# Routed layers whose tails load the experts' rows of the first 512 tokens, normalise them and round the next stage's first weights, with no barriers between the six stages

## What is computed

```python
x = L0_attn_x                                     # (1, 2048, 256)
x = x + 0.5 * _L0_ffn_ref(_layernorm(x, axis=-1), ...)   # stage routed0
x = x + _L0_attn_ref(_layernorm(x, axis=-1), ...)        # stage attention0, one head
x = x + 0.5 * _L0_ffn_ref(_layernorm(x, axis=-1), ...)   # stage routed1
x = x + 0.5 * _L1_ffn_ref(_layernorm(x, axis=-1), ...)   # stage gated0
x = x + _L1_attn_ref(_layernorm(x, axis=-1), ...)        # stage attention1, 16 heads
x = x + 0.5 * _L1_ffn_ref(_layernorm(x, axis=-1), ...)   # stage gated1
```

```python
    eout = jnp.einsum('eci,eih->ech', mid, w_down) * wbuf[..., None]
    y = jnp.zeros((T + 1, h), x.dtype).at[buf.reshape(-1)].add(eout.reshape(-1, h))[:T]
    shared = jax.nn.silu(x @ sw_gate) * (x @ sw_up) @ sw_down
    return (y + shared).reshape(b, s, h)
```

## Time and profile before

| | us |
|---|---|
| median of 3 runs | 2043.96 (2040.21 to 2044.92) |
| the profiled execution: its time, its span | 2039.38, 2037.6 |
| PE, DVE, ACT, POOL busy | 1951.3, 1423.7, 1317.5, 947.1 |
| routed0, attention0, routed1, gated0 end near | 129, 260, 373, 493 |

### The profile page before, as it was taken

One profiled execution on the slowest core, in us unless ns is written; L12 is line 12 of the kernel. 1 busy time (PEld: TensorE's weight loads), 2 busy tenths in 40 slices (PEclk: granted clock), 3 DMA queues, 4 the chain that ended last, 5 costly groups with the idle time before them and its releaser, 6 DMA issues. The chain is left out here.

```text
span 2037.6 us, 40489 instructions
## 1 busy us (share of the span) xinstructions
PE 1951.3 (96%) x13831; PEld 1766.5 (87%) x13831; DVE 1423.7 (70%) x3588; ACT 1317.5 (65%) x3368; POOL 947.1 (46%) x974
## 2 busy tenths in 40 slices
PE   6988989898999999999999999999999999999899
PEld 4767867687899999999999999999999999998788
DVE  8348763545868777786877778787777878777653
ACT  4335633444778687777867777787777778777652
POOL 1642116534455536454553645545365454636242
PEclk9999999999999999999999999999999999999999
DMA  7752057700000000000000000000000000000010
GB/s 251 215 83 32 33 166 211 156 10 9 9 6 9 9 6 4 7 9 9 6 9 6 4 6 9 9 7 9 6 4 7 9 9 7 9 6 1 2 47 32
DMA packets 58602, 73.46 MB, mean 36 GB/s; under 512 B 9760, under 2 KB 45216, under 8 KB 58272
## 3 DMA queue, kind: packets, MB, share of 16 engines
q1 hardware_dynamic: 43808, 53.83, 8.2%
q0 software_dynamic: 14592, 17.04, 5.0%
HBM read 51.06 MB, written 19.80 MB: 35 GB/s over the span
## 5 line engine op out<-in xcount | busy, mean ns | idle before, releaser
L1184 ACT ACTIVATE phase_p<-phase_scores,phase_bias 128x512 f32<-128x512 f32 (+3 forms) x680 | 417.5, 628 | 117.0 <-DVE phase_bias L1172 116.3
L1230 DVE TENSOR_TENSOR phase_pt_lo<-phase_ring,phase_pt_hi 128x512 fp32r<-128x512 f32 (+3 forms) x680 | 390.3, 603 | 89.6 <-ACT phase_pt_hi L1225 85.8
L1225 ACT ACTIVATE phase_pt_hi<-phase_ring 128x512 fp32r<-128x512 f32 (+3 forms) x680 | 342.9, 536 | 106.2 <-PE phase_ring L1210 102.1
L1210 PE MATMUL phase_ring<-sb_ident,phase_p 128*128 128x128 f32 x2312 | 340.8, 274 | 10.8 <-ACT phase_p L1184 4.5
L160 PE MATMUL phase_y<-phase_pt_hi,phase_v_hi 128*128 128x256 f32 (+1 forms) x1152 | 341.5, 296 | 6.6 <-DVE phase_y_lo L2293 6.6
L161 PE MATMUL phase_y<-phase_pt_lo,phase_v_hi 128*128 128x256 f32 (+1 forms) x1152 | 321.5, 279 | 0.0
L162 PE MATMUL phase_y<-phase_pt_hi,phase_v_lo 128*128 128x256 f32 (+1 forms) x1152 | 321.4, 279 | 0.0
L1210 PEld LDWEIGHTS phase_ring<-sb_ident,phase_p 128*128 128x128 f32 x2312 | 272.2, 141 | 51.0 <-ACT phase_p L1184 14.0
L1165 DVE TENSOR_REDUCE phase_peaks<-phase_scores 128x1 f32<-128x512 f32 (+1 forms) x408 | 265.6, 665 | 46.3 <-PE phase_scores L1152 43.8
L2316 POOL TENSOR_TENSOR phase_straight<-phase_rot,late_rope 64x512 f32<-64x512 f32 x128 | 163.7, 1279 | 274.4 <-ACT phase_rot L2188 274.3
L2333 POOL TENSOR_TENSOR sb_x<-sb_x,phase_part 128x512 f32<-128x512 f32 x128 | 164.8, 1288 | 253.5 <-ACT phase_part L2223 247.1
(11 more groups left out here) (272 smaller groups left out, 4857.4 us busy)
## 6 DMA issues: line engine op xcount, KB each, us to landing
phase_e_up<-expert_up SPq DMA_DIRECT2D x32, 352.0 KB, 4.8
phase_e_dn<-expert_down SPq DMA_DIRECT2D x32, 256.0 KB, 5.4
y_rows<-phase_zero SPq DMA_DIRECT2D x16, 512.0 KB, 7.7
sb_x<-y_rows POOLq DMA_DIRECT2D x16, 512.0 KB, 6.6
xn_rows<-phase_ln_xn SPq DMA_DIRECT2D x8, 512.0 KB, 2.9
late_raw_qk<-qk SPq DMA_DIRECT2D x16, 256.0 KB, 2.6
sb_x<-x SPq DMA_DIRECT2D x4, 512.0 KB, 5.7
phase_raw_up<-up SPq DMA_DIRECT2D x8, 256.0 KB, 4.5
```

The lines of the kernel that those rows point to most:

```text
L1184: act.activation(self.p[:, at:at + width], self.scores[:, at:at + width], ACT.Exp, bias=self.bias[:, t % 2:t % 2 + 1], accum_out=self.sums ...
L1210: done = pe.transpose(bank[:, j * P:(j + 1) * P], self.p[:, (4 * place + j) * P:(4 * place + j + 1) * P], self.core.ident[:])
L1225: act.activation(hi, value, ACT.Copy).then_inc(*self.t_hi.one)
L1230: dve.tensor_tensor(lo, value, as_f32(hi), ALU.subtract).then_inc(*self.t_lo.one)
```

## The change

All six stages now go into one Block, so no barrier stands between them. In its place each engine of routed1, gated1 and attention1 waits for the last instructions of the stage before that matter (`follow`: TensorE for ScalarE and VectorE, and for GpSimd too in attention1; the other engines for all). Attention0 and gated0 wait for none of these as a whole.

Behind a routed stage's last expert SyncE loads the next stage's first weights, then rows 0 to 511 of both tables into SBUF rooms (two loads of 512 KB). VectorE adds them to chunk 0 (`grow` 0 and 1), in order before piece 10's and piece 11's `round`; it measures the chunk before piece 11's `round`, scales it behind half-sum (2,0), and TensorE turns it behind the last half-sum. ScalarE, VectorE and (for gated0) GpSimd round the next stage's first weights in the same tail (`ahead`). GpSimd's transfers of chunk 0 are gone, and the six others start with chunk 1. The matmuls without use at the first and third border are gone. In attention0 `values` 0 to 3 come earlier and chunk 1 is turned one tile earlier; in gated0 the side work comes one piece earlier.

```diff
+def follow(engine, prior, *ends):
+    for name in (ends or prior.ends) if prior else ():
+        engine.wait_ge(*prior.ends[name])
...
+        self.y_rooms = [self.e_up[:].rearrange("p s k w -> p (s k w)")[:, b * 4 * H:(b + 1) * 4 * H].rearrange("p (a h) -> p a h", a=4) for b in range(2)]
+        self.y_fetched, self.grown = [core.loads(f"y_fetched{b}") for b in range(2)], sig("grown")
...
+        self.first = ChunkNorm(core, sb, then, (0,), after=lambda c: self.grown[tag, 1], like=self.norm, quick=(0,))
+        self.first_banks = [banks[:, b, :] for b in (6, 7)]
...
-        fill(len(shared))
+        last = NCH * ISM - 1
+        among = {("up", last - 3): [("ahead", 0)], ("round", last - 3): [("ahead", 1)], ("up", last - 2): [("ahead", 2)],
+                 ("round", last - 2): [("ahead", 3)], ("gate", last): [("grow", 0)], ("up", last): [("grow", 1), ("measure",)],
+                 ("sums", NCH - 2, 0): [("scale",)], ("sums", NCH - 1, 1): [("flip", 0), ("flip", 1)]}
+        for steps in shared:
+            for step in steps:
+                order += [step, *among.get(step, ())]
         return order
...
+        self.follower.sp_ahead(sp)
+        sp.wait_ge(*self.e_downed[tag, NE - 1])
+        for b in range(2):
+            sp.wait_ge(*self.placed[b][tag, NE - 2 + b])
+            sp.dma_start(self.y_rooms[b], core.y_rows[b][0:CH, :].rearrange("(t p) h -> p t h", p=P)).then_inc(*self.y_fetched[b].one)
...
+            elif what == "ahead":
+                self.follower.act_ahead(act, *key)
+            elif what == "scale":
+                self.first.act_rows(act, 0)
+            elif what == "flip":
...
+            elif what == "ahead":
+                self.follower.dve_ahead(dve, *key)
+            elif what == "grow":
+                b, x = key[0], core.x[:, 0:4, :]
+                dve.wait_ge(*self.y_fetched[b][tag])
+                dve.wait_ge(*(self.grown[tag, 0] if b else self.added[tag, 0, 1]))
+                dve.tensor_tensor(x, x, self.y_rooms[b], ALU.add).then_inc(*self.grown.one)
+            elif what == "measure":
+                self.first.dve_stats(dve, 0)
+            elif what == "scale":
+                self.first.dve_rows(dve, 0)
+            elif what == "flip":
+                self.first.dve_rest(dve, 0, key[0], self.first_banks[key[0]])
+        self.step.totals[0] += self.steps
...
-        for half, c in GROWN[:3]:
-            if half == 0:
-                pool.wait_ge(*self.added[tag, c, 1])
-            pool.wait_ge(*self.placed[half][tag, NE - 2 + half])
-            pool_grow(core, pool, self.then, half, c)
-GROWN = ((0, 0), (0, 1), (1, 0), (1, 1), (0, 2), (1, 2), (0, 3), (1, 3))
+        self.follower.pool_ahead(pool)
+        pool.wait_ge(*self.y_fetched[0][tag])
+        self.pool_grow(pool, 0)
+        self.first.pool_inverse(pool, 0)
+        pool.wait_ge(*self.placed[1][tag, NE - 1])
+        self.pool_grow(pool, 1)
+    def pool_grow(self, pool, n):
+        half, c = GROWN[n]
+        pool.wait_ge(*self.added[self.tag, c, 1])
+        pool_grow(self.core, pool, self.then, half, c)
...
-    IDLE = {("flip", 0, 0): 22, ("state", 0): 6, ("score", 0, 0, 0): 9, ("score", 0, 1, 0): 5}
...
-        order = [("stats", 0), ("inverse", 0), ("grow", 3), ("grow", 4), ("rows", 0), *project(0)[:2], ("weights", "ws"),
-                 ("weights", "wa"), *project(0)[2:], ("stats", 1), ("weights", "wo0"), ("inverse", 1),
+        order = [("grow", 2), *project(0)[2:], ("values", 0), ("values", 1), ("stats", 1), ("inverse", 1), ("grow", 3), ("bias", 0),
                  ("score", 0, 0, 0), ("peak", 0, 0), ("exp", 0, 0)]
         for t in range(NT + 1):
             nc = t // 4 + 1
             if nc < NCH and t % 4 == 0:
-                order.append(("rows", nc))
-            order += {1: [("grow", 5)], 2: [("grow", 6)], 3: [("stats", 2), ("inverse", 2), ("grow", 7)], 6: [("stats", 3), ("inverse", 3)]}.get(t, [])
+                order += [("rows", nc), ("bias", nc)]
+            order += {1: [("grow", 4)], 2: [("grow", 5)], 3: [("stats", 2), ("inverse", 2)], 6: [("stats", 3), ("inverse", 3)]}.get(t, [])
...
-            if nc < NCH and t % 4 == 1:
+            if nc < NCH and t % 4 == (nc > 1):
                 order += project(nc)[:2]
-            if nc < NCH and t % 4 == 2:
+            if nc < NCH and t % 4 == 1 + (nc > 1):
                 order += project(nc)[2:]
-            if t < NT and t % 2 == 0:
+            if t in (2, 3):
+                order.append(("values", t))
+            if 8 <= t < NT and t % 2 == 0:
                 order.append(("values", t // 2))
...
+    def sp_ahead(self, sp):
         for name in self.names:
             sp.dma_start(self.raw[name], self.core.src[name]).then_inc(*self.weights_in[name].one)
...
+    def act_ahead(self, act, n):
+        if n < len(self.names):
+            name = self.names[n]
+            act.wait_ge(*self.weights_in[name][self.tag])
+            act.activation(self.w_hi[name][:], self.raw[name], ACT.Copy, scale=self.scale(name)).then_inc(*self.weight_hi.one)
...
+    def dve_ahead(self, dve, n):
+        if n < len(self.names):
+            name = self.names[n]
+            dve.wait_ge(*self.weight_hi[name])
+            dve.scalar_tensor_tensor(self.w_lo[name][:], self.raw[name], self.scale(name), as_f32(self.w_hi[name][:]),
+                                     ALU.mult, ALU.subtract).then_inc(*self.weight_lo.one)
...
-                pool_grow(self.core, pool, self.tag, *GROWN[step[1]])
-            elif step[0] == "rows":
+                self.prior.pool_grow(pool, step[1])
...
-            if step in self.IDLE:
-                core.keep_warm(pe, self.y[:], self.IDLE[step])
...
+        act.activation(self.spare[:], self.core.ident[0:1, 0:1], ACT.Exp)
...
-    GROW = {(0, 1): 5, (0, 2): 6, (0, 4): 7}
-    GROWN_NORM = {(0, 2): [("scale", 0, 1)], (0, 3): [("turn", 0, 1)], (1, 1): [("scale", 0, 2)], (1, 2): [("turn", 0, 2)],
-                  (1, 4): [("scale", 0, 3)], (1, 5): [("turn", 0, 3)]}
-    GROWN_LATE = {(0, 5): [("measure", 0, 2), ("invert", 0, 2)], (1, 2): [("measure", 0, 3), ("invert", 0, 3)]}
+    GROW = {(0, 0): 4, (0, 2): 5}
+    GROWN_NORM = {(0, 1): [("scale", 0, 1)], (0, 2): [("turn", 0, 1)], (1, 0): [("scale", 0, 2)], (1, 1): [("turn", 0, 2)],
+                  (1, 3): [("scale", 0, 3)], (1, 4): [("turn", 0, 3)]}
+    GROWN_LATE = {(0, 4): [("measure", 0, 2), ("invert", 0, 2)], (1, 1): [("measure", 0, 3), ("invert", 0, 3)]}
...
+    def sp_ahead(self, sp):
+        for m in range(I1M):
+            self.sp_up(sp, m)
+    def sp_up(self, sp, m):
+        sp.dma_start(self.raw_up[:, :, self.cols(m)], self.core.src["up1"][:, :, self.cols(m)]).then_inc(*self.up_in[m].one)
+    def sp_scales(self, sp):
...
     def sp(self, sp):
         core, src = self.core, self.core.src
-        for m in range(2 if self.ahead else 0, I1M):
-            sp.dma_start(self.raw_up[:, :, self.cols(m)], src["up1"][:, :, self.cols(m)]).then_inc(*self.up_in[m].one)
-            if m == 2:
...
         if self.add_y:
+            self.sp_scales(sp)
             sp.wait_ge(*self.norm.x_in[1][self.tag])
+            follow(sp, self.prior, "pe")
+        else:
+            follow(sp, self.prior)
+            for m in range(2, I1M):
+                self.sp_up(sp, m)
+                if m == 2:
+                    self.sp_scales(sp)
...
-        bank = self.down_ps[:, 0, :]
-        if 0 in self.ahead:
-            self.core.keep_warm(pe, bank, 6)
-        else:
-            self.core.keep_warm(pe, bank, 20)
-            self.pe_turn(pe, 0, 0)
-            self.core.keep_warm(pe, bank, 5)
+        if not self.add_y:
+            follow(pe, self.prior, "act", "dve")
+            self.core.keep_warm(pe, self.down_ps[:, 0, :], 6)
...
+    def act_ahead(self, act, m):
+        self.act_up_weights(act, m)
+    def dve_ahead(self, dve, m):
+        if m < 2:
+            self.dve_up_weights(dve, m)
+    def pool_ahead(self, pool):
+        for m in range(2, 4):
+            self.pool_up_weights(pool, m)
+    def pool_up_weights(self, pool, m):
+        pool.wait_ge(*self.up_w_hi[self.tag, m])
+        pool.tensor_tensor(self.up_lo[:, :, self.cols(m)], self.raw_up[:, :, self.cols(m)], as_f32(self.up_hi[:, :, self.cols(m)]),
+                           ALU.subtract).then_inc(*self.up_w_lo_p.one)
...
         if self.add_y:
-            pool_grow(self.core, pool, tag, *GROWN[3])
-        if not self.ahead:
-            self.norm.pool_inverse(pool, 0)
-            pool.wait_ge(*self.norm.powered[tag, 0])
-        if self.add_y:
-            pool_grow(self.core, pool, tag, *GROWN[4])
-        for m in range(2, I1M):
...
-            if m == 3 and not self.ahead:
-                self.norm.pool_inverse(pool, 1)
+            self.prior.pool_grow(pool, 2)
+            self.prior.pool_grow(pool, 3)
+            self.norm.pool_inverse(pool, 1)
+        else:
+            follow(pool, self.prior)
```

(17 more changed lines are left out.)

178 lines of the change are left out of this document (103 added, 75 removed).

## The result

The changed kernel takes **2045.32 us** (median of 12 runs) where the kernel before takes 2041.08 beside it (12 runs): the ratio is 1.002, 95% interval 1.0011 to 1.0028. So it is about 4 us **slower**; 11.5 us less was forecast, and the range ended at 2042. Its profiled execution took 2045.33 us, with a span of 2043.4, which is 5.8 more than before's 2037.6.

The account below looks back on a forecast made before the run. TensorE was taken as the bound, busy 1951.3 of 2037.6 us. Terms 0.75 + 4.5 + 5.1 + 1.4 + 1.7 - 1.7 = 11.75, forecast as 11.5 off the 2043.96 median, gave 2032.5 us; range 2026 to 2042.

Parts of the forecast that it names:

- Barriers: At the second, fourth and fifth border: a direct wait instead of a barrier saves 0.25 us each, 0.75 us.
- The first border's chain: From routed0's last scatters to attention0's first product: moved into the tail, product at 133.75 instead of 138.11, gain 4.4 us.
- rival 1: Both tails: the new loads take 6.6 us like the accumulating ones, giving 2040.4 us; chance 0.14.
- The stall at half-sum (3,0): In the tail: TensorE, queued behind VectorE's additions and measuring, waits a new 2.3 us.
- Rival 4: Both tails: late loads stop VectorE's ordered steps and TensorE behind; at 10.5 us a load, 2048.2 us; chance 0.07.
- The gain through attention0: Chunk 1's wait and chain end move up by about 4 to 5 us; 4.5 us taken for the first border.
- Rival 2: First border's gain is given back within attention0, chunk 2's rows still being added one after the other; 2037.0 us; chance 0.17.
- The rule on VectorE and GpSimd: Third tail: GpSimd's rounding could hold `grow` 0 by at most 1.1 us; nothing charged; as a rival 2033.6 us, chance 0.06.
- Lowered clock: In the two tails: idle time without the matmuls lowers the clock in one of them, minus 1.7 us (0 to 3.4).
- The third border: gated0's first product at 378.1 instead of 381.51, 3.4 us; with down weights issued earlier, gain 5.1 us there.
- chunk 3: In gated0: the 3.82 us wait before its turns falls to 2.4, gain 1.4 us, and 1.7 of lowered clock is spared.
- The four signs of being wrong: Loads over 5 us, stall at half-sum (3,0) over 4 us, half clock in more than one more stretch, attention0 no shorter.

Follow-up runs that it names:

- apart: Changed kernel with GpSimd's chunk 0 bias addition ahead of chunk 1's measuring, and its rounding behind routed1's last request for rows; 2047.25 us, ratio 1.0017.
- warm: Changed kernel with matmuls without use put back before half-sum (3,0) in two tails and in attention0; 2045.38 us, ratio 1.0012.
- after: The changed kernel itself, against the kernel before; 2045.32 us, ratio 1.002.
- late: Changed kernel with the next stage's weights requested only behind the last expert's down products; 2043.08 us, ratio 1.0002.
- chunk1: apart plus chunk 1 measured, inverted and scaled ahead of chunk 0's values in attention0; 2042.03 us, ratio 1.0010.
- cold6: best6 without the matmuls without use put back in the first three stages; 2037.94 us, ratio 0.9987.
- best6: best4 plus gated0's chunk 1 scaling one piece earlier and its down weights requested earlier; 2031.77 us, ratio 0.9962.
- best: Changed kernel with late, apart and chunk1 together and VectorE's additions placed where their rows land; 2041.17 us, ratio 0.9993.
- bestwarm: best plus some matmuls without use before each tail's first turns and in attention0; 2037.17 us, ratio 0.9980.
- third: Changed kernel with the first border and attention0 put back as before the change; 2041.32 us, ratio 1.0001.
- best4: best2 plus matmuls without use at routed1's opening, and GpSimd's rounding started once chunk 0's rows are scaled; 2034.58 us, ratio 0.9958.
- order: Changed kernel with VectorE's two additions, measuring and scaling moved behind half-sum (2,1)'s addition; 2053.68 us, ratio 1.0048.
- best2: bestwarm with GpSimd's rounding waiting until chunk 0's shift is written in the tail; 2033.69 us, ratio 0.9961.

## Why the prediction was wrong

In the profiles the forecast (11.75 us less before rounding) and the result (5.8 more) are 17.5 us apart. The difference has three large parts, beside small ones of either sign: 8.2 us up to attention0's first product, 3.3 more from there to chunk 1's state, and 6.2 behind gated0's first product, from which to attention1's 107.2 us would follow from the forecast and 113.4 were measured.

- **Barriers: right where it can be seen.** VectorE's last addition in attention0 ends at 267.49 + 0.48 = 267.97 and TensorE goes on at 268.12, 0.15 later (before 0.39). The fifth can't be told: attention1's first product to gated1's takes 1441.96 us instead of 1442.20, and 1441.2 to 1443.3 over the study.

```profile
267.49 0.48 DVE L1581 SCALAR_TENSOR_TENSOR sb_x<-phase_y,phase_inv,sb_x 128x256 f32<-128x256 f32 x1 [1.35 <-PE phase_y L172]
```
```profile
268.12 0.40 PE L170 MATMUL phase_banks<-sb_xt_hi,kept_w_hi 128*16 128x512 f32 x1 [0.67 <-DVE sb_x L1581]
```

- **The first border's chain: the step that cost most, wrong by 8.2 us** (141.97 instead of 133.75; 138.11 before). Its terms: expert 15's load was issued 2.1 us later, by chance as far as the profiles tell; the scatters came another 2.5 later, of which about 1.8 is the weights' request. The step that failed there counted the weights' roundings and put at nothing **SyncE's new loads, in a stretch where the transfer engines were already 89 to 98% busy** (98 to 104 us before the change). After the change the windows read (the last but one number is the DMA share; before, it was 0.04 from 104 to 106):

```profile
102.00:104.00 2.00, 1.86 (x9) 0.98 (x7) 0.48 (x1) 0.50 (x3) 0.67 (x2) 1.00 1.02 304
104.00:106.00 2.00, 1.64 (x9) 1.40 (x10) 0.34 (x1) 0.68 (x3) 1.08 (x1) 1.00 0.85 265
106.00:108.00 2.00, 2.00 (x14) 1.66 (x13) 0.00 (x0) 0.62 (x2) 0.00 (x0) 1.00 0.91 192
```

From the last scatter to the landing of the odd rows took 10.3 us instead of 8.0 (8.3 in apart and warm): 6.0 until the load could be issued, for which 4.4 was forecast, and 4.2 for the load. From there to the product took 13.6 instead of 12.3, above all since half-sums (3,0) and (3,1) ran mostly at half clock (6.6 us instead of 4.1). The loads themselves took 4.2 us, 0.7 over the estimate: rival 1 is out. The chain as such works, for with the clock at full it took 20.7 us from the last scatter (warm), 20.2 were forecast.
- **The stall at half-sum (3,0): mis-sized.** 6.03 us instead of 2.3. Its end hangs on the odd rows: (3,0) starts 4.4 us behind their landing in every run with this order (after, late, apart, chunk1; forecast: 4.6), since VectorE's addition of them and the measuring stand ahead of what TensorE needs. Rival 4 had that mechanism but priced only slow loads; the scatters ahead of them were late too.
- **The gain through attention0: wrong by another 3.3 us.** I expected chunk 1's wait and the end of its chain to move up by about the same 4 to 5 us. From first product to chunk 1's state took 19.1 instead of 15.8 us. That is GpSimd's bias addition, moved right behind chunk 1's power, holding a 128x4 step (shown by apart: 15.7). Without it the order still keeps 4 us: the values now stand ahead of the measuring of rows that had long landed (shown by chunk1: 11.6). Rival 2 had the gain given back in attention0, but by chunk 2's rows; from chunk 1's state to routed1's first product took only 1.2 us more than before.
- **The rule on VectorE and GpSimd: weighed, and priced at the wrong place.** The Trainium skill, SBUF — State Buffer, section Who interferes with whom, says that a VectorE instruction with two SBUF inputs and a GpSimd instruction that reads SBUF contend. The trace agrees, and shows the size: VectorE's step ends when GpSimd's instruction does (152.52 + 3.48 = 156.00, 153.11 + 2.86 = 155.97), so the short step pays for the long one. I took 1.1 us from a 256-wide subtraction and looked only at the third tail. There GpSimd's rounding ended before the rows landed, as I said, but it held a 128x512 subtraction of VectorE for 3.26 us (at 367.51; 0.66 elsewhere).
- **Lowered clock: wrong, 1.7 us charged.** Half clock lasted 34 us in the profile where it was 14 before. I took the matmuls without use as work that only fills idle time. Two comparisons, each on one chip, show what they are worth: 5 to 6 us (cold6, best6) and 3 to 4 us (best, bestwarm).
- **The third border: right at the border, wrong behind it.** Last scatter to gated0's first product was forecast as 21.2 and took 20.2 us (third: 20.2; before 24.6). Against routed1's first product it came 3.5 us sooner, as forecast, in spite of 1.7 for the scatters. What should have followed (1.7 by the down weights, 1.4 and 1.7 at chunk 3) did not: the wait for chunk 3 fell to 2.42 as forecast, but chunk 1's turns now wait 3.57 us, since its inverse and scaling stand behind a down weight's rest in VectorE's order, and ScalarE waits 2.43 us for that weight's load; half clock follows. The down weights are issued at 385.86, not at the 377.0 of the forecast, though relative to routed1's first product that is 4.6 us sooner than before. Where these orders are mended, the next to be late are the down weights, then chunk 1's rows (best4, best6), which are both transfers. No profile of the study has less than 110.9 us (warm, chunk1) from gated0's first product to attention1's.

The four signs of being wrong that the prediction named came out as: loads under 5 us; stall over 4 us; half clock in more stretches; attention0 no shorter from its first product on. The second came (6.03 us), and so did the fourth: 126.2 us to routed1's first product instead of 121.7. The third came in length (34 us against 14), not by count: five stretches against four, only one more. The loads stayed under 5 us.

What stays open: why expert 15's load varies by 3.5 us between profiles; why warm gained so little; why order's clock is so low; which of best2 to best6 is the fastest, since their intervals overlap; and whether the clock at routed1's opening falls by chance, as it seems.

The fastest versions have ratios of 0.9945 to 0.9962: 8 to 11 us under the kernel before, with the change's plan, its orders mended and some matmuls without use back.

## What to carry to other kernels

A step moved into another stage's tail must be placed in every engine's order at the time when its data lands; if it stands earlier on an in-order engine, whatever that engine feeds waits too, until the data has landed (here 4.4 us beyond it). Count what a move issues (loads in a stretch already full of transfers) and what it lands beside (GpSimd from SBUF beside short VectorE steps), not only what it removes. Matmuls without use at a border held the clock up here and were worth 3 to 6 us in two pairs of runs (in warm, no gain that can be told): take them out only once the idle time itself is gone.

## What the runs showed of the hardware

- While GpSimd's bias addition or rounding ran from SBUF, VectorE's 128x4 step with two inputs in SBUF was held until it ended (0.16 became 3.48, 3.50 and 3.66 us), and so was the scaling of rows (0.74 became 3.60 and 3.96). Instructions that read PSUM beside it were not held (sums 0.64, rests 0.65 us). Neither was the measuring, though all its tensors are in SBUF: it has one input, and took 0.41 us as elsewhere at 410.56 of the changed kernel, beside a GpSimd subtraction from 410.47 to 411.80.
- The length of a wait didn't tell that of the half clock around it: some 10 us with order's wait of 4.49 us before the turns, some 7 with the changed kernel's 6.03 before (3,0).
- Waits of nearly the same length (1.0 to 1.2 and 1.4 to 1.6 us at routed1's opening) were followed by 10 to 14 us of half clock in 7 profiles of 14 and by full clock in 6.
- Plain loads of 512 KB issued by SyncE took 4.1 to 4.5 us from issue to landing in the changed kernel, GpSimd's accumulating loads of that size 5.9 to 9.9 (median 6.5).
